# Two attention phases of a fused transformer block: three pieces of TensorE's order moved next to pieces of their own kind

## What is computed

```
def _attn(xq, xc, Wq, Wk, Wv, Wo, bo):
    q = (xq @ Wq).reshape(B, N, HEADS, D_HEAD)
    k = (xc @ Wk).reshape(B, S, HEADS, D_HEAD)
    v = (xc @ Wv).reshape(B, S, HEADS, D_HEAD)
    attn = softmax(einsum('bnhd,bshd->bhns', q, k) * scale)
    out = einsum('bhns,bshd->bnhd', attn, v).reshape(B, N, HEADS * D_HEAD)
    return out @ Wo + bo

x = _attn(_ln(x, g1, b1), _ln(x, g1, b1), Wq1, ...) + x
x = _attn(_ln(x, g2, b2), context, Wq2, ...) + x
x = _geglu_ff(_ln(x, g3, b3), Wp, bp, Wf, bf) + x
```

## Time and profile before

| | us |
|---|---|
| median of 3 runs | 463.78 (463.76 to 464.13) |
| the profiled execution | 464.39 |
| its span, first to last instruction | 462.7 |

### The profile page before, as it was taken

One profiled execution on the slowest core, in us unless ns is written; L12 is line 12 of the kernel. 1 busy time (PEld: TensorE's weight loads), 2 busy tenths in 40 slices (PEclk: granted clock), 3 DMA queues, 4 the chain that ended last, 5 costly groups with the idle time before them and its releaser, 6 DMA issues.

```text
span 462.7 us, 17536 instructions
## 1 busy us (share of the span) xinstructions
PE 448.1 (97%) x7574; PEld 408.1 (88%) x7574; DVE 354.1 (77%) x642; ACT 322.5 (70%) x598; POOL 199.0 (43%) x219
## 2 busy tenths in 40 slices
PE   7989999999999999999999999999999999999897
PEld 6969898898998989989889899898999787777797
DVE  4899778778786787877877778696885678889572
ACT  5676776877778768877787777855545577776763
POOL 2584432555354634544353433531442232132583
PEclk9999999999999999999999999999999999999999
DMA  7102020310200000000000000000000000000011
GB/s 225 35 23 64 22 81 3 77 47 4 61 4 12 1 11 11 3 11 1 13 11 1 11 3 11 2 3 3 1 0 10 18 10 20 0 2 1 10 37 47
DMA packets 17301, 10.57 MB, mean 23 GB/s; under 512 B 7888, under 2 KB 16272, under 8 KB 17232
## 3 DMA queue, kind: packets, MB, share of 16 engines
q1 hardware_dynamic: 16800, 9.48, 7.4%
q10 hardware_dynamic: 432, 0.07, 0.1%
HBM read 8.50 MB, written 1.05 MB: 21 GB/s over the span
## 4 chain that ended last, share of the span: by engine, by line
PE 85%; DVE 9%; ACT 3%; issue 1%; DMA 1%; POOL 1%; DVEq 0%; SPq 0%
PE stage L606 12%; PE stage L608 11%; PE stage L607 11%; PE scp L697 7%; PE scp L772 7%; PE scp L921 6%; PE scp L742 6%; PE out0p L792 4%; PE out0p L818 3%; PE out0p L793 3%; PE out0p L794 3%; PE stage L756 2%; PE scp L713 2%; PE stage L621 1%; DMA pr<-in_L_xattn_Wq_dram 1%
## 5 line engine op out<-in xcount | busy, mean ns | idle before, releaser
L1464 POOL TENSOR_TENSOR pr<-pr,rc 128x1024 f32<-128x1024 f32 x32 | 60.2, 1903 | 71.3 <-DVE rc L1255 71.3
L1007 ACT ACTIVATE pr<-pr 128x1024 f32<-128x1024 f32 x48 | 50.7, 1056 | 34.4 <-DVE pr L1225 26.5
L1405 POOL TENSOR_TENSOR rstd<-veps,neghalf 128x2 f32<-128x2 f32 x32 | 22.4, 700 | 85.6 <-DVE veps L1173 85.4
L945 ACT ACTIVATE vt<-stage 64x512 f32<-64x512 f32 x80 | 47.3, 591 | 11.4 <-PE stage L608 8.9
L1220 DVE TENSOR_REDUCE mx<-scp 128x16 f32<-128x1024 f32 x32 | 39.2, 1224 | 11.5 <-PE scp L697 11.0
L1273 DVE COPY pt<-scp 128x512 f32<-128x512 f32 x32 | 22.1, 692 | 32.0 <-PE scp L742 31.8
L1268 DVE TENSOR_TENSOR ot_r<-scp,ot_h 128x512 fp32r<-128x512 f32 x64 | 41.1, 685 | 6.0 <-ACT ot_h L945 4.4
L945 ACT ACTIVATE ot_h<-scp 128x512 fp32r<-128x512 f32 x64 | 34.8, 598 | 12.5 <-PE scp L772 12.5
L945 ACT ACTIVATE q_of_heads<-stage 128x512 f32<-128x512 f32 x62 | 35.3, 596 | 10.2 <-PE stage L608 8.4
L945 ACT ACTIVATE k_of_heads<-stage 128x512 f32<-128x512 f32 x62 | 37.1, 600 | 5.4 <-PE stage L608 0.3
L1253 DVE TENSOR_REDUCE sm<-pr 128x16 f32<-128x1024 f32 x32 | 38.7, 1210 | 2.4 <-ACT pr L1007 2.4
(11 more groups left out here) (254 smaller groups left out, 1408.7 us busy)
## 6 DMA issues: line engine op xcount, KB each, us to landing
ctx_in<-in_ctx_dram SPq DMA_DIRECT2D x16, 96.0 KB, 2.0
masked_k<-in_L_xattn_Wo_dram SPq DMA_DIRECT2D x2, 512.0 KB, 4.2
out_dram<-rows SPq DMA_DIRECT2D x8, 128.0 KB, 1.8
rows<-in_x_dram SPq DMA_DIRECT2D x1, 768.0 KB, 9.3
pr<-in_L_xattn_Wq_dram SPq DMA_DIRECT2D x1, 512.0 KB, 4.8
pr<-in_L_xattn_Wk_dram SPq DMA_DIRECT2D x1, 512.0 KB, 6.4
pt<-in_L_xattn_Wv_dram SPq DMA_DIRECT2D x1, 512.0 KB, 7.6
rows<-in_L_xattn_Wq_dram SPq DMA_DIRECT2D x1, 512.0 KB, 3.7
```

The costliest lines, as they stand in the source:

```text
L945: return nc.scalar.activation(dst, s, ACT.Copy)
L1007: nc.scalar.activation(pr[t][:, :], pr[t][:, :], ACT.Exp, scale=scale[s.phase]).then_inc(exped, 1)
L1464: nc.gpsimd.tensor_tensor(halves(pr[t][:, :]), halves(pr[t][:, :]), rc[:, t, :, None].to_broadcast([ROWS, H, N]), ALU.mult).then_inc(probs, 1)
```

## The change

Three pieces move, in SELF and CROSS:

- V's last product of `one` is made at the end of group `s`, behind the eight Q and K products of `two`, no longer in its own group between the two turns of P. The first group's is made ahead of the loop with the other three.
- Both turns of P then stand in one run.
- Wo's result of a group is turned back in the next group, just ahead of x's transposes, and VectorE adds it to the rows there, between its two `av_step`s. The last group of CROSS turns back the result of the group before it there, and its own where it did before.

In the very first group ScalarE copies both halves of V's product 0. In the group before the last of CROSS, V's last product stands ahead of GEGLU's. Every engine's order and the tables of counts follow:

```diff
@@ def copiers
     if kind == "val":
-        return (2, 0) if i == 2 else (1, 1)
+        return (2, 0) if i == 2 or (p, g, i) == (SELF, 0, 0) else (1, 1)
@@ TensorE, def group
-                    if one.phase == GEGLU:
-                        val_step(s, (3,))
-                        turn_step(s, 0)
-                    else:
-                        turn_step(s, 0)
-                        val_step(s, (3,))
+                    before = s.before()
+                    turn_step(s, 0)
                     turn_step(s, 1)
                     av_step(s, 0)
+                    if before:
+                        out_turn_step(before)
                     x_step(two, s)
                     av_step(s, 1)
@@
                     if two.phase == GEGLU:
+                        val_step(one, (3,), s)
                         p_step(two, s, (0, 1))
-                        out_turn_step(s)
                     else:
-                        proj_step(two, s, range(2))
-                        out_turn_step(s)
-                        proj_step(two, s, range(2, 8))
+                        proj_step(two, s)
+                        val_step(one, (3,), s)
@@ TensorE, ScalarE and VectorE, ahead of the groups
-            val_step(Step(SELF, 0), range(3))
+            val_step(Step(SELF, 0), range(4))
@@ ScalarE, def group
-                        pt_step(s, 0)
-                        val_step(s, (3,))
+                    pt_step(s, 0)
                     pt_step(s, 1)
@@
                     if two.phase == GEGLU:
+                        val_step(one, (3,))
                         exp_step(one, 1)
@@
                         p_step(two, range(2, 8))
+                        val_step(one, (3,))
@@ VectorE, def group
-                        pt_step(s, 0)
-                        val_step(s, (3,))
+                    before = s.before()
+                    pt_step(s, 0)
                     pt_step(s, 1)
                     stats_step(three)
                     av_step(s, 0)
+                    if before:
+                        out_step(before)
                     av_step(s, 1)
@@
                     for t in range(T):
                         sum_step(one, t)
-                    out_step(s)
+                    val_step(one, (3,))
```

More of the change, by code:

```diff
@@ L102, in __init__ @@
         self.p(SELF, 1)
-        self.vals(SELF, 0, range(3))
+        self.vals(SELF, 0, range(4))
         for p in range(PHASES):
@@ L162, in group @@
                 self.turned(p, g, t)
-            self.vals(p, g, (3,))
             for i in (0, 1):
@@ L175, in group @@
             elif two.phase == GEGLU:
+                self.vals(one.phase, one.first, (3,))
                 self.p(two.phase, two.first, (0, 1))
```

## The result

The changed kernel takes 472.78 us, median of 4 runs (471.20 to 473.36), against 463.83 us of the kernel before on the same chip: 1.018 times as long, 95% interval 1.0167 to 1.0193. Slower was right; 465.9 us, with a range up to 466.9, was not. Most of what was missed is one stop of TensorE that no step of the prediction had.

The account below looks back on a forecast made before the run. TensorE, busy 97% of 462.7 us, was taken as the clock. Terms 0.2 (turning back) + 1.7 (Q/K product 5) + 1.0 (AV) - 0.8 (start) = +2.1 us on 463.8 gave 465.9 us, range 464.6 to 466.9.

Parts of the forecast that it names:

- turning back, its own length: Wo's two transposes, moved ahead of x's transposes: 0.22 us out and in cancel 14 times, 15 put in, net +0.2 us.
- V's last product: Moved to the end of the Q/K run: its 3 matmuls cost 0.70 us before and after, so zero.
- AV behind VectorE's copy: AV of tile 0 waits for VectorE's copy of P's transposes: stall of 0.07 us a group, 1.0 us in all.
- Q/K product 5: Sixth Q/K product waits for ScalarE's copy of product 2: 0.12 us a group, 1.7 us in all, bounds 1.0 and 3.1.
- start: First group: one VectorE copy less ahead of AV, scores and `veps` earlier: -0.8 us, bounds 0 and -0.9.
- a longer new wait: Rival: an unseen wait, such as P's second turn behind GpSimd, 1.4 us per 0.1 us a group, above 467; chance 0.07.
- the joins buy nothing: Joining transposes or products into longer runs on TensorE saves no time, as changes of kind cost none and no drain goes.
- the 0.15 us that a start behind several semaphores takes: TensorE starts 0.15 us after a copy ends if several semaphores precede the product; applied to AV's first product, with four.
- the 0.05 us behind a single one: TensorE starts 0.05 us after a copy ends if it waits for one semaphore; applied to the sixth Q/K product.
- `veps` escapes GpSimd: In the first group VectorE reaches `veps` before GpSimd's operation starts, so the 0.4 us that the scores lost goes.

Follow-up runs that it names:

- the later loads: Load of wp and the three loads behind it put one exponential later: changed kernel 469.95 us, kernel before 464.16 us.
- the same line of code: Kernel before, ScalarE copying both halves of V's product 0 in the very first group: 462.59 us with the later loads, 462.99 us with its own.

## Why the prediction was too low

| step | predicted | measured |
|---|---|---|
| turning back, its own length | +0.2 us | the stretch of four transposes is 111.76 - 111.17 = 0.59 us, against 88.53 - 88.16 = 0.37 before: 0.22 in, 0.22 out |
| V's last product | 0 | 127.16 - 126.46 = 0.70 us, no wait |
| AV behind VectorE's copy | 1.91 us after the first transpose, +1.0 | 1.91 us; without the turning back, groups of 18.74 us: +1.0 to 1.1 |
| Q/K product 5 | 14 x 0.12 = +1.7 us | 14 x 0.22 = 3.1 us, of which 0.12 + 0.10 a group |
| start | -0.8 us | -0.73 us in the profile; `veps` 0.62 us, forecast 0.2 to 0.5 |
| other | 0 | the stop 4.16, other late blocks 0.2 |

**The step that failed** is one that is not there: "14 of them between the start and the last one" look alike, so I multiplied one group. The groups did not look alike. Two of the kernel before are 0.14 and 0.43 us too long, and I read over them. In the first, AV of tile 1 lasts 1.27 us instead of 1.16 around the first instruction of block 11; in the second the trace shows the wait:

```profile
88.53 1.27 PE L772 MATMUL scp<-pt,vt 64*64 64x64 f32 x64
...
240.67 0.27 PE L772 MATMUL scp<-pt,vt 64*64 64x64 f32 x1 [0.19 <-issue]
```

They are places where the program itself arrives late. The order with fewer long matmuls in that row paid more for the same event (2.7 against 0.6 us with the later loads), and the changed program met `wp`'s load there. None of the rivals had this mechanism; "a longer new wait" was meant for GpSimd. With 4.4 us of it the forecast would have been about 470.3, and with the 1.4 us of product 5 below 471.7, against 463.8 + 8.0 = 471.8 by the profile.

**The term that was mis-sized** is product 5. Its start was right to 0.01 us (0.05 us behind the copy), but I counted the late start alone. A product that starts late behind its copy has its second matmul 0.22 us behind the first, not 0.12 (124.20 and 124.42; 101.66 and 101.88; 102.34 and 102.56): so the change gave back the whole 0.22 us that it took out. The rows for this were in the profile: product 5 at 44.93 us had its first matmul at 0.39 us instead of 0.28, and I even named it, as a reason for the start. The bound of 3.1 us that I gave for this term was the result, and my range for the sum did not reach to it. The Trainium skill, page "TensorE: Matmul & The Clock Gate", section Single matmul latency, gives a matmul on its own a fixed time besides its columns, of issue and of the drain through the array. No run here shows whether that is what makes the second matmul late.

**What held.** That the joins buy nothing (the stretches add up as 0.11 us a transpose and 0.23 us a matmul), the 0.15 us that a start behind several semaphores takes and the 0.05 us behind a single one, and that `veps` escapes GpSimd. At the start both time and engine were right. The row of AV names ScalarE's copy of P, but that is the copy that ended last, tile 1's; tile 0's ended, by the length of one, at 29.02 + 0.60 = 29.62 us. The first of VectorE's two copies ends at 29.37 + 0.69 = 30.06 us, TensorE's semaphore instruction for it (L767) starts at 30.10 and AV at 30.21, 0.15 us behind the copy; forecast were 30.10 and 30.25. What the prediction did not see is that V's last product, made ahead of the loop, puts a second copy of V before P's on VectorE. Without that move the same line of code puts the first group's scores at 34.14 us instead of 35.04, and the kernel 1.6 us ahead of the one before.

That the direction was right owes nothing to the larger part of the loss, 4.4 us, which the prediction did not have; its own terms came out as 0.2 + 3.1 + 1.0 - 0.7 = 3.6 us of slowdown, and so carried the direction by themselves.

**What stays open.** Why a block is asked for just where it is. With the later loads, the changed order had it 2.8 us behind the first transpose in SELF's group 3 and 2.9 us in the long group of CROSS, the order before 1.5 us behind in the one and 0.35 us ahead in the other; what triggers it is not in the profile. It is not only that the stock is used up faster: in the group of CROSS the transfer itself began with 106 instructions left ahead of the block in the changed order and with 274 left in the order before, both with the later loads. And no run of its own splits the 3.2 us that the loads add into waiting for the transfer (1.7 us of idle time, 0.65 against 2.33) and the lower clock after it (some 1.4 us).

## What to carry to other kernels

Before one group's stall is multiplied by the number of groups, list the lengths of all groups: those that stand out show what is not in the order, here the arrival of the program itself, and a change that makes rows of short instructions denser can pay more there, as this one did. The wait of product 5 cost its idle time and a late second matmul, 0.12 + 0.10 us, so taking work out from between products whose copies are just in time gave back all that it took. And a transfer that is "hidden" can lie in the way of TensorE's own program: shift large loads, or shift the blocks, and time again before judging an order by one build.

## What the runs showed of the hardware that I had not expected

- TensorE's program comes in packets of 16 KB on a DMA queue of its own, one for 256 of its instructions; in SELF and CROSS a packet takes 0.9 to 1.7 us. The first instruction of a late one ran 2.2 to 2.8 us after the transfer had started (225.69 to 227.92, 89.58 to 91.97, 222.38 to 225.21 us). 64 pieces of AV with their weight loads, half a block, run in 1.1 us.
- Behind a load of 512 KB such a packet came 1.9 us later than with that load moved away (89.58 against 87.65 us). The Trainium skill, page "Runtime: NRT & Kernel Launch", section The launch sequence, says that instruction fetch is autonomous and needs no instruction. The trace agrees in that no instruction of the kernel issues these packets, but they are not free of the DMA traffic.
- After 2.33 us without work the granted clock was 0.52 in the next 2 us of the profiled execution (the mean of one of the four runs, 1.000, shows hardly any such stretch); after stops of 0.65 and 0.95 us it stayed at 1.00.
- 16 calls of a 64x64 matmul into the same place (32 matmuls in the trace) took 2.1 us, 0.13 us a call, where the 32 calls of one tile's AV, in different places, take 1.1 us.
